# Input sides of channel mixing and of the gated layer as 2x2 block products of seven products each, gate kept in DRAM

## The reference

```
y = norm(x)                                  # first norm; then the block _L0_attn_ref on y:
h = ln1(y);  hh = h shifted by one token
r, k, v = (h*mix + hh*(1-mix)) @ Wr.T, Wk.T, Wv.T
x1 = y + (sigmoid(r) * wkv(k, v)) @ Wo.T     # state starts empty, no recurrence over tokens
h = ln2(x1); hh = h shifted by one token
kk = (h*cm_mk + hh*(1-cm_mk)) @ Wkey.T       # 512 -> 2048     "channel mixing, input side"
kv = silu(kk) @ Wval.T                       # 2048 -> 512     "output side"
sr = sigmoid((h*cm_mr + hh*(1-cm_mr)) @ Wcr.T)
x2 = x + x1 + sr * kv
z = norm(x2)
gate, up = split(z @ w_gate_up.T)            # 512 -> 2 x 2048 "gated layer, input side"
out = x2 + (silu(gate) * up) @ w_down.T      # 2048 -> 512     "output side"
```

## Time and profile before

| | us |
|---|---|
| median of 3 runs | 1176.63 |
| lowest, highest run | 1175.46, 1176.77 |
| span of the profiled execution | 1174.3 |
| TensorE busy in it | 1132.1 |
| VectorE, GpSimd, ScalarE busy | 602.0, 455.7, 336.5 |

### The profile page before, as it was taken

One profiled execution on the slowest core, in us unless ns is written; L12 is line 12 of the kernel. 1 busy time (PEld: TensorE's weight loads), 2 busy tenths in 40 slices (PEclk: granted clock), 3 DMA queues, 4 the chain that ended last, 5 costly groups with the idle time before them and its releaser, 6 DMA issues.

```text
span 1174.3 us, 13753 instructions
## 1 busy us (share of the span) xinstructions
PE 1132.1 (96%) x4992; PEld 931.6 (79%) x4992; DVE 602.0 (51%) x895; ACT 336.5 (29%) x575; POOL 455.7 (39%) x348
## 2 busy tenths in 40 slices
PE   6789999979999999999999999999999999999998
PEld 4667778767888888888888888888888888888887
DVE  8998999998344544454459822222222222222223
ACT  4465632345322222222223321122111211112111
POOL 6756466567432333333243413332132321333201
PEclk9889899989999999999999999999999999999999
DMA  6011112440100000100010000000010001000002
GB/s 235 1 37 37 72 37 72 72 69 22 45 19 27 27 19 26 27 27 18 27 41 23 18 27 27 28 21 26 18 36 18 27 18 27 27 27 18 1 36 108
DMA packets 23271, 43.61 MB, mean 37 GB/s; under 512 B 2112, under 2 KB 2240, under 8 KB 23232
## 3 DMA queue, kind: packets, MB, share of 16 engines
q1 hardware_dynamic: 21120, 38.89, 10.7%
q0 software_dynamic: 2112, 4.19, 2.2%
HBM read 38.88 MB, written 4.19 MB: 37 GB/s over the span
## 4 chain that ended last, share of the span: by engine, by line
PE 80%; DVE 13%; issue 2%; POOL 2%; ACT 2%; DMA 0%; DVEq 0%; SPq 0%; ACTq 0%
PE bank L234 26%; PE bank L236 26%; PE bank L235 26%; DVE made L817 4%; DVE made L811 3%; POOL operand L1048 1%; DVE resid L787 1%; DVE resid L843 1%; PE bank L288 1%; DVE bank L835 1%; POOL weights L1048 1%; DVE resid L846 1%; DVE moments L772 1%; DVE feat L878 0%; ACT operand L501 0%
## 5 line engine op out<-in xcount | busy, mean ns | idle before, releaser
L234 PE MATMUL bank<-operand,weights 128*128 128x512 f32 x832 | 324.0, 389 | 1.8 <-DVE made L854 1.8
L236 PE MATMUL bank<-operand,weights 128*128 128x512 f32 x832 | 323.7, 389 | 0.0
L235 PE MATMUL bank<-operand,weights 128*128 128x512 f32 x832 | 323.7, 389 | 0.0
L234 PE MATMUL bank<-weights 128*128 128x512 f32 x576 | 225.8, 392 | 8.1 <-ACT feat L567 6.7
L1077 POOL TENSOR_TENSOR weights<-made,weights 128x512 fp32r<-128x512 f32 x64 | 82.3, 1306 | 368.1 <-ACT weights L571 368.1
L235 PE MATMUL bank<-weights 128*128 128x512 f32 x576 | 225.0, 391 | 0.0
L236 PE MATMUL bank<-weights 128*128 128x512 f32 x576 | 224.9, 390 | 0.0
L921 DVE TENSOR_TENSOR made<-bank,made 128x512 f32<-128x512 f32 x64 | 44.2, 692 | 307.6 <-ACT made L646 307.6
L234 PEld LDWEIGHTS bank<-operand,weights 128*128 128x128 f32 x832 | 156.1, 188 | 35.0 <-DVE made L854 2.6
L235 PEld LDWEIGHTS bank<-operand,weights 128*128 128x128 f32 x832 | 156.1, 188 | 32.5
L236 PEld LDWEIGHTS bank<-operand,weights 128*128 128x128 f32 x832 | 156.2, 188 | 32.4
(11 more groups left out here) (69 smaller groups left out, 1042.8 us busy)
## 6 DMA issues: line engine op xcount, KB each, us to landing
staging<-wts SPq DMA_DIRECT2D x92, 256.0 KB, 2.6
feat<-x SPq DMA_DIRECT2D x4, 1024.0 KB, 5.1
resid<-x POOLq DMA_DIRECT2D x4, 1024.0 KB, 9.1
resid<-x SPq DMA_DIRECT2D x3, 1024.0 KB, 10.4
out<-resid SPq DMA_DIRECT2D x3, 1024.0 KB, 4.4
feat<-wts SPq DMA_DIRECT2D x8, 256.0 KB, 6.5
resid<-x SPq DMA_DIRECT2D x4, 256.0 KB, 3.8
out<-resid SPq DMA_DIRECT2D x4, 256.0 KB, 2.5
```

The costliest lines, as they stand in the source:

```text
L234: pe.matmul(acc, left(0), right(0), start=first, stop=False)
L235: pe.matmul(acc, left(0), right(1), start=False, stop=False)
L236: return pe.matmul(acc, left(1), right(0), start=False, stop=last)
```

## The change

Both input sides are now made for a pair of blocks (1024 tokens) at a time as a 2x2 block product: left are 2 x 2 weight blocks of 128 inner features by 256 input features (two k tiles), right 2 x 2 input blocks of 256 features by 512 tokens. Seven products of 6 matmuls each stand for the eight of before (Winograd's form, with 4 sums on the left and 4 on the right). The left factors are A11, A12, A22, S1 to S4, the right ones B11, B21, B22, T1 to T4.

- A key unit (16: 8 for each pair) makes 256 inner features for 1024 tokens; a gate unit (32: 16 for each pair) makes 128 gate and 128 up features for 1024 tokens. All 48 units are written out. PSUM: banks X, Y, V, Z (B) hold the products, A[0..3] the output pieces.
- Products 1 and 7 start fresh. ScalarE copies X to Y and V to `seventh`; products 6, 5, 3 go on in Y, 2 in X, 4 in Z, which VectorE seeds with Y + seventh; V becomes Y + seventh after product 5.
- The weights come as 4 quarters of 128x256 (512 KB a unit), VectorE makes the 4 left sums, ScalarE the high part (in two wide copies), GpSimd the low part. The output-side weights come as 256 KB tiles, split in the same way.
- The right factors are made once per stage (4: keys and gates of each pair) in the last unit of the stage before: 8 VectorE sums, 14 ScalarE high parts, 14 VectorE low parts. For the first stage this happens in the entry.
- An output half is one block by 256 inner features, 4 pieces of 6 matmuls; the pieces are put between the products (`some`). A key unit runs the two halves of the unit before, a gate unit one half. VectorE adds each piece onto the residual tile (in channel mixing too, without the gate).
- x1 + x and the gate of each block are stored to DRAM (8 transfers of 1 MB); after a pair's keys VectorE reads them back a token tile at a time and makes x2 (`make_x2`), then norm3, whose transposes lie in units 11, 14, 19 and 23.
- In the entry the first halves of cr and ck are ScalarE's (`rest_of_cr`, `rest_of_ck`), ck of blocks 2 and 3 moves into unit 0. The queue orders at the entry's end change.

The core of it (PE, ACT, DVE and GpSimd are the functions `unit` in this order):

```diff
+def halves_in(u):
+    if u == 0:
+        return ()
+    if u < KEYS:
+        return (2 * (u - 1), 2 * (u - 1) + 1)
+    return (u + KEYS - 2,)
+def inner_tiles_by(h):
+    g, b = divmod(h, 2)
+    if g < KEYS:
+        return 4 * g + 2 * b + 2
+    return 4 * KEYS + 4 * (g - KEYS) + 2 + b + 1
...
+            def product(acc, u, a, c, fresh):
+                if stage_start(u):
+                    pe.wait_ge(combo_lo, 2 * (SEVEN * stage_of(u) + MADE_ORDER.index(c) + 1))
+                wts_of = left[u % 2]
+                for k in range(2):
+                    hi, lo = (wts_of[:, part, a, k * P:(k + 1) * P] for part in range(2))
+                    pe.matmul(acc[:], hi, combo[:, c, k, 0, :], start=fresh and k == 0, stop=False, skip_group_check=True)
+                    pe.matmul(acc[:], hi, combo[:, c, k, 1, :], start=False, stop=False, skip_group_check=True)
+                    mm = pe.matmul(acc[:], lo, combo[:, c, k, 0, :], start=False, stop=k == 1, skip_group_check=True)
+                return mm
...
+            def out_half(h, s):
+                g = h // 2
+                n = SUBS * h + s
+                if s == 0:
+                    pe.wait_ge(inner_lo, inner_tiles_by(h))
+                    pe.wait_ge(right_lo, 2 * g + 2)
+                after = [j for j in range(BLOCKS) if NORM3_AFTER[j] <= n < NORM3_AFTER[j] + SUBS]
+                if after:
+                    pe.wait_ge(t3_kept, SUBS * after[0] + s + 1)
+                elif n >= SUBS:
+                    pe.wait_ge(added, n - SUBS + 1)
+                else:
+                    pe.wait_ge(h2_ready, KT * BLOCKS)
+                for i in range(2):
+                    mm = three_passes(A[s][:], lambda p: inner[:, h % 3, i, p, s * P:(s + 1) * P],
+                                      lambda p: right[:, g % 2, i, p, :], i == 0, i == 1)
+                mm.then_inc(out_psum, 1)
...
+            def unit(u):
+                pieces = [(h, s) for h in halves_in(u) for s in range(SUBS)]
+                share = len(pieces) // 4
+                def some(n):
+                    for h, s in pieces[share * n:share * (n + 1)]:
+                        out_half(h, s)
+                pe.wait_ge(left_lo, 2 * u + 1)
+                if u:
+                    pe.wait_ge(silu_done, silu_by(u - 1, 0))
+                else:
+                    pe.wait_ge(sr_ready, SUBS * (BLOCKS - 1) + 1)
+                product(X, u, A11, B11, True).then_inc(p1, 1)
+                pe.wait_ge(left_lo, 2 * u + 2)
+                if u == 0:
+                    pe.wait_ge(sr_ready, SUBS * (BLOCKS - 1) + 3)
+                elif is_key(u - 1):
+                    pe.wait_ge(silu_done, silu_by(u - 1, 2))
+                else:
+                    pe.wait_ge(gated, 2 * (u - KEYS))
+                product(V, u, S3, T3, True).then_inc(p7, 1)
+                some(0)
+                pe.wait_ge(x_copied, u + 1)
+                product(Y, u, S2, T2, False).then_inc(p6, 1)
+                product(X, u, A12, B21, False).then_inc(p2, 1)
+                some(1)
+                pe.wait_ge(z_seeded, u + 1)
+                product(Y, u, S1, T1, False).then_inc(p5, 1)
+                some(2)
+                product(Z, u, A22, T4, False).then_inc(p4, 1)
+                pe.wait_ge(v_summed, u + 1)
+                product(Y, u, S4, B22, False).then_inc(p3, 1)
+                some(3)
+                for j in range(BLOCKS):
+                    if u == NORM3_UNIT[j]:
+                        norm3(j)
...
+            def gated_hi(u):
+                for b in range(2):
+                    n = 2 * (u - KEYS) + b
+                    act.wait_ge(gated, n + 1)
+                    inner_hi_tile(4 * KEYS + n, 2 * chunk_of(u) + b, u % 2)
...
+            def unit(u):
+                after = stage_of(u + 1) if u + 1 < UNITS and stage_start(u + 1) else None
+                act.wait_ge(p1, u + 1)
+                if u:
+                    act.wait_ge(silu_done, silu_by(u - 1, 3 if is_key(u - 1) else 1))
+                else:
+                    act.wait_ge(sr_ready, SUBS * BLOCKS)
+                act.activation(Y[:], X[:], ACT.Copy).then_inc(x_copied, 1)
+                if after is not None:
+                    combo_hi_of(after, B11)
+                act.wait_ge(p7, u + 1)
+                if u:
+                    act.wait_ge(v_summed, u)
+                act.activation(seventh[:], V[:], ACT.Copy).then_inc(seventh_copied, 1)
+                if u == 0:
+                    rest_of_ck(2)
+                if u > KEYS:
+                    gated_hi(u - 1)
+                if after is not None:
+                    combo_hi_of(after, T3)
+                if u + 1 < UNITS:
+                    unit_left_hi(u + 1, 0)
+                unit_right_hi(u)
+                if after is not None:
+                    combo_hi_of(after, T2)
+                if u == 0:
+                    rest_of_ck(3)
+                if u + 1 < UNITS:
+                    unit_left_hi(u + 1, 1)
+                act.wait_ge(p2, u + 1)
+                if is_key(u):
+                    key_tile(u, 0, X)
+                else:
+                    gate_tile(u, 0, X)
+                if after is not None:
+                    combo_hi_of(after, B21)
+                    combo_hi_of(after, T1)
+                if is_key(u):
+                    act.wait_ge(p4, u + 1)
+                    key_tile(u, 1, Z)
+                    act.wait_ge(v_summed, u + 1)
+                    key_tile(u, 2, V)
+                act.wait_ge(p3, u + 1)
+                if is_key(u):
+                    key_tile(u, 3, Y)
+                else:
+                    gate_tile(u, 1, Y)
+                if after is not None:
+                    combo_hi_of(after, T4)
+                    combo_hi_of(after, B22)
+                for j in range(BLOCKS):
+                    if u == NORM3_UNIT[j]:
+                        norm3(j)
             act.wait_ge(vec_loaded, 16)
             early_hi(ITEM_R, ROW_R)
...
+            def sums(u):
+                dve.wait_ge(quart_loaded, 16 * (u + 1))
+                dve.tensor_tensor(quart[:, 4, :], quart[:, 0, :], quart[:, 3, :], ALU.add).then_inc(sums_done, 1)
+                dve.tensor_tensor(quart[:, 6, :], quart[:, 1, :], quart[:, 0, :], ALU.subtract).then_inc(sums_done, 1)
+                dve.wait_ge(sums_done, 4 * u + 1)
+                dve.tensor_tensor(quart[:, 5, :], quart[:, 4, :], quart[:, 1, :], ALU.subtract).then_inc(sums_done, 1)
+                dve.wait_ge(sums_done, 4 * u + 3)
+                dve.tensor_tensor(quart[:, 7, :], quart[:, 2, :], quart[:, 5, :], ALU.subtract).then_inc(sums_done, 1)
...
+            def seed(u):
+                dve.wait_ge(p6, u + 1)
+                dve.wait_ge(seventh_copied, u + 1)
+                if u == 0:
+                    dve.wait_ge(sr_ready, SUBS * BLOCKS)
+                elif is_key(u - 1):
+                    dve.wait_ge(silu_done, silu_by(u - 1, 1))
+                dve.tensor_tensor(Z[:], Y[:], seventh[:], ALU.add).then_inc(z_seeded, 1)
+            def sum_v(u):
+                dve.wait_ge(p5, u + 1)
+                dve.tensor_tensor(V[:], Y[:], seventh[:], ALU.add).then_inc(v_summed, 1)
+            def gate(u, b):
+                n = 2 * (u - KEYS) + b
+                dve.wait_ge(silu_done, silu_by(u, b))
+                if b == 0:
+                    dve.wait_ge(p4, u + 1)
+                else:
+                    dve.wait_ge(v_summed, u + 1)
+                tile = made_at(4 * KEYS + n)
+                dve.tensor_tensor(tile, (Z, V)[b][:], tile, ALU.mult).then_inc(gated, 1)
...
+            def unit(u):
+                after = stage_of(u + 1) if u + 1 < UNITS and stage_start(u + 1) else None
+                pieces = [(h, s) for h in halves_in(u) for s in range(SUBS)]
+                share = len(pieces) // 4
+                def some(n):
+                    for h, s in pieces[share * n:share * (n + 1)]:
+                        accumulate(h, s)
+                if after is not None:
+                    right_sums(after)
+                some(0)
+                if after is not None:
+                    combo_lo_of(after, B11)
+                    make_t2(after)
+                seed(u)
+                if u == 0:
+                    mix_ck(2)
+                if u + 1 < UNITS:
+                    sums(u + 1)
+                if after is not None:
+                    combo_lo_of(after, T3)
+                for j in range(BLOCKS):
+                    if u == FIN_UNIT[j]:
+                        make_x2(j, (0, 1))
+                    if u == FIN_UNIT[j] + 1:
+                        norm3_stats(j)
+                some(1)
+                if after is not None:
+                    combo_lo_of(after, T2)
+                sum_v(u)
+                if u == 0:
+                    mix_ck(3)
+                some(2)
+                for j in range(BLOCKS):
+                    if u == FIN_UNIT[j]:
```

(72 more changed lines are left out.)

777 lines of the change are left out of this document (380 added, 397 removed).

## The result

The changed kernel takes **1232.91 us**, the median of 4 runs (1230.59 to 1234.63); the kernel before took 1176.14 (1175.46 to 1176.77) beside it. The ratio is 1.0478, 95% interval 1.0461 to 1.0494: 4.8% slower. The forecast was 1180, with a range of 1162 to 1207. The direction was right, by little: the forecast had 0.3% and a chance of 0.49 for slower. The size and the range were wrong. The profiled execution has a span of 1232.2 us and an own time of 1234.13.

A forecast was written before the change was run, and what follows sets the result against it. TensorE, busy 96% of 1174.3 us, was taken as the bound. Removed matmuls (-65.3) and added waits (+43.5, 1.5, 0, 6.5, 5, 7, 5.5) summed to +3.7: span 1178.0, time 1180 us, 0.3% slower, range 1162 to 1207.

The forecast's parts named there:

- The chain: Gate units 18 to 46, every second: first output piece waits for bank copy, high part, low part; 15 times 2.9 us, +43.5.
- the clock falls in them: Sign of being wrong: granted clock falls in the gate-unit gaps, where the forecast had 1.00 from unit 1 on.
- the clock falls in the new gaps: Rival, slower: each 2.9 us gap brings the clock down, about 2.1 us lost, +32, giving 1212; chance 0.13.
- the waits in units 0 and 1: Term for products waiting on VectorE and ScalarE in the first two units: +6.5 us (3 to 11).
- The matmuls: Term for the input sides: 288 matmuls removed at 0.2267 us each, -65.3 us.
- the gap isn't there: Rival, faster: the gate units' wait for the low part was misread and is absent, giving 1137; chance 0.06.
- The entry: Term for the stretch before unit 0: 0 us (-8 to +8), product 1 of unit 0 near 292.
- x2 in the gate units: Units 17 and 21: VectorE's 8 added operations and readback, then statistics and norm3 in the next unit; +5.5 us (0 to 10).
- the ends of the key stages: Units 7 and 15: VectorE's 14 low parts and 8 sums delay the V sum, +5 us for two (0 to 16).
- x2 in the key units: Units 9 and 12: the room of 20.4 us takes VectorE's x2 work, nothing added.
- VectorE late in every gate unit: Rival, slower: half-size sums held by GpSimd's low parts delay the V sum, 0.5 us in 31 units, 1195; chance 0.13.
- The stated tests: Trace signs: 4704 matmuls, 15 gaps near 2.9 us, named VectorE waits, clock 1.00 from unit 1, unit 0 near 292.

The follow-up runs named there:

- experiments 2 and 3: Against the changed kernel: product 6 moved ahead of the first output piece in 15 gate units, 1194.27 us; 11 overwritten matmuls before each of those 15 pieces, 1212.47 us.
- experiment 1: Changed kernel with ScalarE making a gate unit's two high parts at that unit's end, ahead of its waits for products 1 and 7: 1165.21 us.
- experiment 6: Changed kernel with the early high parts, plus product 1 computed twice in each of the 48 units (288 matmuls put back): 1222.06 us.
- experiment 4: Changed kernel with VectorE normalising block 3 ahead of mix_ck(1), the sums of unit 0 and mix_cr(2): 1222.41 us.

## Why the prediction was wrong, step by step

**The failed step is the clock behind the gaps.** The chain, its place, its 15 times and its length were right (2.72 for 2.9 us; its bounds were added up too wide, since the 0.52 and 1.47 that they name give 2.8 and 3.1). For the clock the prediction took nothing, since it had been 1.00 through a gap of 1.54 and since the gaps "stand between dense stretches". That was the argument that failed: 2.56 us of idleness between dense stretches gave half the clock 14 times of 15, at 1.75 us each, and it is the idleness that gives it (experiments 2 and 3). The prediction's own sign of being wrong, "the clock falls in them", was met. Its rival, "the clock falls in the new gaps", had the mechanism and a price of 32 us, 2.1 for each, for a loss that came as 24.5; it had a chance of 0.13. Length alone does not decide it: in the changed kernel the wait of 2.14 us in unit 7 brought the clock down, and the one of 2.11 in unit 15 did not. The trace of the kernel before had a case nearer than 1.54, 2.34 us idle until 220.92 with the clock at 1.00 behind it; it would have spoken for the same step. The other 13 us of slow matmuls lie behind the waits in units 0 and 1, at the stage ends and at x2; experiment 1, without the 15 gaps, still has 11.9.

**The matmuls** were worth their 65.3 us (experiment 6). The change pays as soon as nothing makes TensorE stand: experiment 1 takes the gap away and has 1165. The rival "the gap isn't there" gave 1137 for that, with every other term as forecast; the difference is the 6 us of the entry, some 13 of other waits (38.1 for the 25.5 of the forecast sum without its 43.5) and 12 of slow matmuls, 31 for the 30 between the spans.

**The entry** was set at 0 between -8 and +8, and cost 6.3. The walk of the queues had the time at which the normalisation starts to half a microsecond. It used 1.92 us for it, from the earlier trace rows; it took 6.27, beside GpSimd's low parts, which ran from 259.31 to 265.48 (the pair of rows in experiment 4), and the left part that GpSimd made behind them until 267.43.

**x2 and the stage ends.** x2 in the gate units was sized 7 us too small, the ends of the key stages 3, and x2 in the key units cost 3 where nothing was forecast. The order of the work was read rightly, and its durations not. The rows of the changed kernel in unit 17:

```profile
664.85 2.06 DVE L1091 TENSOR_TENSOR quart<-quart 128x256 f32<-128x256 f32 x1
...
669.98 2.36 POOL L1348 TENSOR_TENSOR left<-quart,left 128x1024 fp32r<-128x1024 f32 x1 [1.91 <-ACT left L741]
670.05 2.84 DVE L1148 TENSOR_TENSOR resid<-resid,fin 128x512 f32<-128x512 f32 x1
...
674.13 0.69 DVE L1173 TENSOR_TENSOR bank<-bank,e 128x512 f32<-128x512 f32 x1
...
674.87 0.50 PE L406 MATMUL bank<-combo,left 128*128 128x512 f32 x1 [4.51 <-DVE bank L1173]
```

An addition of 512 columns took 2.84 us beside a GpSimd operation of 1024, and 0.69 without one; the sum took 0.90 as the worst from the earlier trace rows. A weight sum of 256 columns took 2.06 where 0.45 was used, and the next one, at 666.84, took 1.51. Together these three take 4.9 us more than their 0.42, 0.42 and 0.69 alone, and the V sum behind them is 4.5 us late. No run took GpSimd's work away from beside them, so this part rests on the rows.

The 0.90 was not the worst that the kernel before had to show. The operation at 62.61 met only the last 0.35 us of GpSimd's two, and the same line 2.57 us earlier, beside the whole of the first, took 1.78:

```profile
59.96 3.00 POOL L1031 TENSOR_TENSOR weights<-staging,weights 128x512 fp32r<-128x512 f32 x2
60.04 1.78 DVE L843 TENSOR_TENSOR resid<-resid,e 128x512 f32<-128x512 f32 x1
```

So the price that was used here, and as the argument against the rival "VectorE late in every gate unit", came from an operation that had met little of it.

The Trainium skill, SBUF - State Buffer (Who interferes with whom), calls the port pair that VectorE and GpSimd share an exclusive lock. The trace agrees more than the 0.90 of the earlier trace rows let expect: the VectorE addition at 670.05 ends 0.55 us after the GpSimd operation at 669.98, as if it had been held throughout.

**The rival "VectorE late in every gate unit"** did not come: beyond the units named, the V sum is late nowhere in the gate stage. Experiment 1 shows 443 matmuls in 100 us there.

**The stated tests.** Right: 4704 matmuls; the gaps, their ender and their units; V sum waits in units 0, 7, 15 and 31; waits for the gating in units 18 and 22, and in unit 32 one of 1.21 us that the profile calls "issue". Wrong: the clock at 1.00 from unit 1 on; product 1 of unit 0 near 292. Not foreseen: the V sum late in units 9 and 12.

## What to carry to other kernels

An idle stretch of TensorE has two prices, its length and what the clock takes behind it; look in the trace for idle stretches of the length that the change makes, and where none lies near, put the fall into the sum with a chance of its own, and the whole of it into the bound. Then look at which engine queue the late operand stands in: here two instructions, put behind a wait that they did not need, cost 67.7 us, more than all the matmuls saved. When VectorE is given two-operand work in SBUF beside wide GpSimd operations, price it at the GpSimd operation's duration, and expect each mended wait to show the next one in the queue.

## What the runs showed of the hardware

- Idle stretches of TensorE and the granted clock, from unit 2 on in the ten profiled executions of the changed kernel and its variants: of 76 stretches of 1.15 to 1.92 us none brought 0.50; of 14 of 2.11 to 2.15 us, 6 did; of 39 of 2.40 to 2.57 us, 30; of 6 of 2.79 to 2.90 us, 3; all 18 of 3.36 us and more did. What decides between 2.1 and 2.9 us is not shown. A fall mostly took 8 matmuls (0.43 us each), 1.75 us lost, and at times twice as long.
- Matmuls that do nothing for the output held the clock at 1.00 in all 15 waits: 165 of them made the kernel 20.4 us faster.
- VectorE operations with two SBUF inputs, alone and at the longest, as these two groups of the changed kernel (ns: shortest, median, longest) show; with GpSimd at 1.9 us for 768 columns and 2.4 for 1024.

```profile
L1148 DVE TENSOR_TENSOR resid<-resid,fin x16: 680/772/2897, 498.7 to 757.3; 128x512 f32<-128x512 f32 x16
...
L1091 DVE TENSOR_TENSOR quart<-quart x48: 409/420/2060, 256.6 to 1193.2; 128x256 f32<-128x256 f32 x48
```

- An operation that reads one wide SBUF tensor was held too: the normalisation's four tensor_scalar took 6.27 us beside GpSimd's work and 1.92 without it (experiment 4).
